# Routed stage: another order for the first layer's activations, the router's exponentials and the gated sums

## The chip, the core and the metric

One NeuronCore of a Trainium2 chip runs the whole program. The metric is the device time of one execution in microseconds (us), as the median of several executions.

## The reference

Two transformer layers run one after the other on 2 x 1024 rows of 256 numbers. Everything up to the last part (two attentions, a sparse feed-forward part) is untouched here. The last part, which the kernel calls the routed stage, is this:

```python
xr = layernorm(x).reshape(-1, D)
route_probs = softmax(xr @ wr.T)              # 8 experts
routes_k, indices_k = top_k(route_probs, 2)
gates = routes_k / sum(routes_k)
h = silu(xr @ w1.T)
h = silu(h @ w3.T)
h = h @ w2.T
out = zeros_like(xr)
for k in range(2):
    out = out.at[indices_k[:, k]].add(gates[:, k:k + 1] * h)
x = x + out
```

The indices name experts 0 to 7 and are used as row numbers of `out`, so that only its first 8 rows get anything: each is a sum over all rows, weighted by the gates.

## The kernel before

Rows are handled in 16 tiles of 128, four tiles to a chunk of 512, so there are four chunks (`d.NC`, the last one is `LAST`). Each stage is written by hand as one instruction list per engine; the lists meet only through semaphores, and each engine takes its own list strictly in order. So what sets the order of the work is the order of the calls in each engine's function. A wait holds up everything behind it on that engine.

Products in reduced-precision fp32 are made from a high part and a low part of each operand: three matmuls (high by high, high by low, low by high) stand for one. ScalarE (ACT) makes a high part by copying, VectorE (DVE) makes the low part by subtracting.

The stage before (`stage_queries`) has already normed, turned and split chunks 0 to 2 and prepared the weights. `stage_routed` (line 2116) has these pieces:

- `last_rows` (DVE) norms the last chunk; `turn_last` (TensorE, PE) transposes it into `ps_2` with 8 transposes; ACT copies the two halves to the high part (line 2263), `last_low` (DVE, line 2189) makes the low part.
- `route(c)` (PE) makes the router's 8 columns for four tiles: 6 matmuls of 8 columns for each tile. For chunks 0 to 2 it takes two matmuls of layer 1 (`layer1_terms`, line 2329, 512 columns) ahead of each tile, which makes the 24 of chunks 0 and 1. `route(LAST)` has no such matmuls between, and waits for the last chunk's low part (`lo_ok`).
- The router's softmax: DVE takes the maximum and subtracts it (lines 2241 and 2242, after all four `route` calls, `l_ps`), ACT makes the exponentials (line 2266, waits `lmax_ok`), and DVE goes on with `shares` (sums, quotients, the 8 largest), `places` (their positions) and `gates`, which releases `g_ok`.
- Layer 1 of a chunk: 12 matmuls on PE, then ACT applies Silu to each half (line 2274) and copies the high part (line 2276), then `low_h(c)` on DVE (line 2198). The buffers are double, by `c % 2`.
- Layer 2 of a chunk: 24 matmuls of 256 columns on PE, which wait for the low halves (`hl_ok`); ACT applies Silu from `ps_2` (line 2282), which releases `h2_ok`.
- `add_up(c)` (PE): four products of the gates with layer 2's rows (line 2359), all chunks summed into one bank `ps_a`. Then comes a short tail: a copy, two transposes, the product with w2, the addition to the first 8 rows and their way out.

ACT needs a table for each kind of function; changing it is an instruction of its own (`ACT_TABLE_LOAD`), which the compiler puts ahead of the first function that needs it. `warm` is an exponential of one column, whose result nobody uses, placed so that the exponentials' table is there early.

Of the kernel before, what the change touches and what calls it, by code (L numbers as in the profile page):

```python
# [23 lines left out]
P = 128  # L24
# [2091 lines left out]
def stage_routed(nc, d, io, keep, out):  # L2116


    with ExitStack() as ctx:
# [19 lines left out]
        acc = st.sb("acc", [NE, d.E])  # L2139
        acc_t = st.sb("acc_t", [P, d.KT, NE])  # L2140
        w = NormWork(st, TPC)
        warm = st.sb("warm", [P, 1])
        ps_th = [st.ps(f"ps_th{i}", [P, d.KT, d.CH]) for i in range(2)]
        ps_2 = st.ps("ps_2", [P, 2, d.CH])
        ps_l = st.ps("ps_l", [P, d.NT, NE])
# [4 lines left out]
            st.sem(n) for n in ("h_ps", "h1_ok", "hh_ok", "hl_ok", "l_ps", "lmax_ok", "ex_ok"))  # L2150
        h2_ps, h2_ok, g_ok, a_ps = st.sem("h2_ps"), st.sem("h2_ok"), st.sem("g_ok"), st.sem("a_ps")

        acc_ok, fin_ok, warm_ok = st.sem("acc_ok"), st.sem("fin_ok"), st.sem("warm_ok")
        out_tiles = out.rearrange("b (t p) e -> p (b t) e", p=P)
        HALVES = TPC // 2

        with nc.Block() as block:
# [12 lines left out]
            def _(dve):  # L2170
# [15 lines left out]
                def last_low():  # L2186
                    for k in range(d.KT):
                        dve.wait_ge(hi_ok, k + 1)
                        nc.vector.tensor_tensor(turned_rows(d, keep, 1, k, LAST * d.CH, d.CH), ps_2[:, k, :],  # L2189
                                                as_f32(turned_rows(d, keep, 0, k, LAST * d.CH, d.CH)),  # L2190
                                                ALU.subtract).then_inc(lo_ok, 1)

                def low_h(c):
                    if c >= 2:
                        dve.wait_ge(h2_ps, HALVES * (c - 1))
                    for m in range(d.KT):
                        dve.wait_ge(hh_ok, d.KT * c + m + 1)
                        nc.vector.tensor_tensor(h_lo[:, c % 2, m, :], h1[:, c % 2, m, :],  # L2198
                                                as_f32(h_hi[:, c % 2, m, :]), ALU.subtract).then_inc(hl_ok, 1)

                def spread(ap, n):
                    return ap.unsqueeze(2).to_broadcast([P, d.NT, n])
# [33 lines left out]
                last_rows()  # L2236
                dve.wait_ge(iota_ok, 1)
                nc.vector.tensor_copy(iota_f[:], iota_i[:])
                last_low()
                dve.wait_ge(l_ps, d.NC)  # L2240
                link(nc.vector.tensor_reduce(lmax[:], ps_l[:], AX.X, ALU.max))
                nc.vector.tensor_tensor(lg[:], ps_l[:], spread(lmax[:], NE), ALU.subtract).then_inc(lmax_ok, 1)
                shares()
                low_h(0)
                places()
                low_h(1)
                gates()
                for c in range(2, d.NC):
                    low_h(c)
                dve.wait_ge(a_ps, 1)  # L2250
                nc.vector.tensor_copy(acc[:], ps_a[0:NE, 0:d.E]).then_inc(acc_ok, 1)  # L2251
                dve.wait_ge(a_ps, 2)
# [4 lines left out]

            @block.scalar
            def _(act):
                norm_root(nc, act, w, 1)  # L2260
                for k in range(d.KT):
                    act.wait_ge(t_ps, k + 1)
                    nc.scalar.activation(turned_rows(d, keep, 0, k, LAST * d.CH, d.CH), ps_2[:, k, :], ACT.Copy).then_inc(hi_ok, 1)  # L2263
                nc.scalar.activation(warm[:], w.sd[:, 0:1], ACT.Exp, scale=0.0).then_inc(warm_ok, 1)
                act.wait_ge(lmax_ok, 1)
                nc.scalar.activation(ex[:], lg[:], ACT.Exp).then_inc(ex_ok, 1)  # L2266

                def layer1(c):
                    for m in range(d.KT):
                        act.wait_ge(h_ps, d.KT * c + m + 1)  # L2270
                        if c >= 2:
                            act.wait_ge(hl_ok, d.KT * (c - 1))
                            act.wait_ge(h2_ps, HALVES * (c - 1))
                        nc.scalar.activation(h1[:, c % 2, m, :], ps_th[c % 2][:, m, :], ACT.Silu).then_inc(h1_ok, 1)  # L2274
                        act.wait_ge(h1_ok, d.KT * c + m + 1)
                        nc.scalar.activation(h_hi[:, c % 2, m, :], h1[:, c % 2, m, :], ACT.Copy).then_inc(hh_ok, 1)  # L2276

                def layer2(c):
                    for j in range(HALVES):
                        act.wait_ge(h2_ps, HALVES * c + j + 1)  # L2280
                        t = TPC * c + 2 * j
                        nc.scalar.activation(h2[:, t:t + 2, :].rearrange("p t e -> p (t e)"), ps_2[:, j, :], ACT.Silu)\
                            .then_inc(h2_ok, 1)

                layer1(0)
                for c in range(d.NC):
                    if c + 1 < d.NC:
                        layer1(c + 1)
                    layer2(c)

            @block.tensor
            def _(pe):
# [69 lines left out]
                        ins.then_inc(a_ps, 1)  # L2362

                wide = itertools.chain(layer1_terms(0), layer1_terms(1))
                for c in range(LAST):
                    route(c)
                turn_last()
                route(LAST)
                for c in range(d.NC):
                    if 2 <= c + 1 < d.NC:  # L2370
                        layer1(c + 1)
                    layer2(c)
                    if c:
                        add_up(c - 1)
                add_up(d.NC - 1)
                pe.wait_ge(acc_ok, 1)
                for k in range(d.KT):
                    ins = nc.tensor.transpose(flat_l[:, k * NE:(k + 1) * NE], acc[:, k * P:(k + 1) * P],
# [77 lines left out]
```

## Time and profile before

| what | value |
|---|---|
| median of 3 runs | 1232.25 us (1230.89 to 1232.38) |
| the profiled execution's own time | 1228.95 us |
| its span | 1227.1 us |
| mean granted TensorE clock over the span | 0.958 |
| PE busy | 1083.5 us (88%) |
| DVE busy | 911.0 us (74%) |
| ACT busy | 628.5 us (51%) |
| routed stage, from its first matmul at 1171.08 us to the end of the span | 56 us |

All durations below are of the profiled execution. The time ahead of and behind the span is 1228.95 - 1227.1 = 1.85 us. Times of an instruction are counted from the start of the span. PE is the matrix engine's multiplication, which is pipelined: the record of a matmul is longer than its distance to the next one, so that distances from start to start are used. The granted clock is the share of the full TensorE clock (2.4 GHz) that the chip granted in a stretch: 1.00 is 2.4 GHz and 0.50 is 1.2 GHz.

### The profile page before, as it was taken

The page shows a single profiled execution, that of the slowest core. Times are in us where ns is not written, and L with a number is a line of the kernel's source. Part 1 is how long each engine was busy: PE and PEld are TensorE (multiplying, and loading weights), DVE is VectorE, ACT ScalarE, POOL GpSimd, SP SyncE. Part 2 cuts the span into 40 slices and gives each one's busy share as a digit, 9 for nine tenths or more (in the row PEclk, how much of TensorE's full clock was granted, in tenths as well). Part 3 has the DMA queues.
Part 4 walks back from the last instruction along what each step waited for, and adds up shares of the span by engine and source line. Part 5 has one row for each costly group of instructions (what it writes and reads, how often), then busy time and mean ns, then how long its engine had stood idle before and what let it go on. Part 6 is the DMA issues. An engine that isn't in the chain of part 4 may idle for free. (4 is left out here: it accounts for less than half of the span.)

```text
span 1227.1 us, 18400 instructions
## 1 busy us (share of the span) xinstructions
PE 1083.5 (88%) x7034; PEld 749.2 (61%) x7034; DVE 911.0 (74%) x1698; ACT 628.5 (51%) x1098; POOL 218.8 (18%) x173
## 2 busy tenths in 40 slices
PE   2979999999999987777867889999997899999978
PEld 2823333333333346666756768888886689888966
DVE  7778999999999604689898886565553878897833
ACT  2526878788787863775651223333333433433323
POOL 6004500000000001000033303000000744644400
PEclk9969999999999998998988999999997999999989
DMA  2771133033030010000000020110101000000010
GB/s 94 228 219 28 27 54 50 5 53 53 8 48 2 2 40 1 1 0 1 1 18 1 1 83 25 35 36 18 35 1 61 1 1 1 1 1 1 1 65 5
DMA packets 24850, 40.02 MB, mean 33 GB/s; under 512 B 3116, under 2 KB 12344, under 8 KB 24760
## 3 DMA queue, kind: packets, MB, share of 16 engines
q1 hardware_dynamic: 24760, 38.82, 13.2%
q8 instruction: 56, 0.92, 0.3%
q14 instruction: 34, 0.28, 0.1%
HBM read 28.06 MB, written 10.49 MB: 31 GB/s over the span
## 5 line engine op out<-in xcount | busy, mean ns | idle before, releaser
L668 DVE TENSOR_REDUCE att_mx<-att_ps_m 128x2 f32<-128x1024 f32 x256 | 310.9, 1225 | 23.3 <-PE att_ps_m L562 19.8
L651 ACT ACTIVATE att_prob<-att_ps_s 128x512 f32<-128x512 f32 x512 | 278.3, 596 | 80.3 <-PE att_ps_s L590 67.7
L606 PE MATMUL att_ps_o<-att_prob,v_rows 128*32 128x256 f32 (+1 forms) x1920 | 159.4, 405 | 0.0
L1885 POOL TENSOR_TENSOR qry_prod<-qry_qr,lin_ksum 128x512 f32<-128x512 f32 x64 | 93.1, 1457 | 302.7 <-ACT qry_qr L2006 291.5
L590 PE MATMUL att_ps_s<-qst,kst 50*128 50x512 f32 x512 | 127.9, 495 | 13.6 <-ACT att_prob L651 12.6
L590 PEld LDWEIGHTS att_ps_s<-qst,kst 50*128 50x128 f32 x512 | 48.1, 183 | 127.1 <-ACT att_prob L651 117.4
L562 PE MATMUL att_ps_m<-kst,qst 48*128 48x512 f32 x512 | 110.0, 424 | 8.7 <-DVE att_mx L668 7.0
L2006 ACT ACTIVATE qry_qr<-qry_ps_q 128x512 f32<-128x512 f32 x64 | 38.3, 599 | 132.4 <-PE qry_ps_q L153 118.9
L153 PE MATMUL qry_ps_o<-qry_m,qry_n_hi 128*128 128x256 f32 x512 | 98.6, 291 | 0.9 <-DVE qry_n_lo L1915 0.8
L1596 DVE SCALAR_TENSOR_TENSOR key_k_lo<-kf_ps,key_k_hi 128x512 fp32r<-128x512 f32 x64 | 44.2, 690 | 61.6 <-ACT key_k_hi L1674 61.0
L606 PEld LDWEIGHTS att_ps_o<-att_prob,v_rows 128*32 128x32 f32 x1920 | 38.1, 108 | 84.3 <-ACT att_prob L651 71.2
L153 PEld LDWEIGHTS qry_ps_o<-qry_m,qry_n_hi 128*128 128x128 f32 x512 | 77.7, 188 | 2.3 <-issue 1.8
L153 PE MATMUL qry_ps_o<-qry_m,qry_n_lo 128*128 128x256 f32 x256 | 71.3, 279 | 0.0
L1674 ACT ACTIVATE key_k_hi<-kf_ps 128x512 fp32r<-128x512 f32 x64 | 38.1, 597 | 62.6 <-PE kf_ps L153 55.4
L562 PEld LDWEIGHTS att_ps_m<-kst,qst 48*128 48x128 f32 x512 | 50.6, 193 | 22.4 <-DVE att_mx L668 18.4
L1915 DVE TENSOR_TENSOR qry_n_lo<-qry_ps_t,qry_n_hi 128x512 fp32r<-128x512 f32 x64 | 44.3, 691 | 24.3 <-ACT qry_n_hi L1995 22.5
L1905 DVE SCALAR_TENSOR_TENSOR qry_qn<-qry_rec,qry_qr 128x512 f32<-128x512 f32 x64 | 55.1, 861 | 2.2
L850 POOL MEMSET mlp_ones<- 128x128 f32 x1 | 0.2, 210 | 313.0 <-POOLq L502 313.0
L153 PE MATMUL kf_ps<-key_k_hi,kf_xk 128*128 128x512 f32 x128 | 45.9, 399 | 5.5 <-DVE key_k_lo L1596 5.5
L1900 DVE TENSOR_REDUCE qry_nrm<-qry_prod 128x8 f32<-128x512 f32 x64 | 43.7, 683 | 9.2 <-POOL qry_prod L1885 7.1
L153 PE MATMUL qry_ps_q<-qry_w_hi,kf_xt 128*128 128x512 f32 x128 | 47.2, 413 | 3.3 <-DVE qry_w_lo L1964 3.3
L1350 PE MATMUL kf_ps<-mlp_wp,ident 128*128 128x256 f32 x152 | 44.5, 456 | 5.4 <-ACT mlp_ws_t L1184 5.4
(409 smaller groups left out, 2330.2 us busy)
## 6 DMA issues: line engine op xcount, KB each, us to landing
qst<-qk_parts SPq DMA_DIRECT2D x48, 128.0 KB, 4.3
kst<-qk_parts SPq DMA_DIRECT2D x48, 128.0 KB, 6.5
qk_parts<-att_out SPq DMA_DIRECT2D x16, 256.0 KB, 4.5
qk_parts<-qk_lo SPq DMA_DIRECT2D x16, 256.0 KB, 4.6
residual<-L_attn_x SPq DMA_DIRECT2D x4, 512.0 KB, 5.9
lin_wq_raw<-L_attn_Wv SPq DMA_DIRECT2D x4, 512.0 KB, 3.6
lin_wq_raw<-L_attn_Wq SPq DMA_DIRECT2D x4, 512.0 KB, 5.5
lin_wq_raw<-L_attn_Wo SPq DMA_DIRECT2D x4, 512.0 KB, 3.9
```

What stands on the lines that cost most here:

```text
L153: ins = nc.tensor.matmul(out, a, b, start=first and n == 0, stop=last and n == len(terms) - 1)
L562: ins = nc.tensor.matmul(ps_m[:, n % 2, r, :], qst[g % RING][rows, v % NB, j, t * P:(t + 1) * P], kst[g % RING][rows, j, half * d.CH:(half ...
L590: ins = nc.tensor.matmul(ps_s[:, (n + r) % BANKS, :], kst[g % RING][rows, j, s * P:(s + 1) * P], qst[g % RING][rows, t, j, :], start=True, ...
L606: ins = nc.tensor.matmul(ps_o[32 * h:32 * h + 32, cols], vall[:, NS * b + s, h0 + h, :], prob[:, u % PR, h, cols], start=s == 0, stop=s == ...
L651: nc.scalar.activation(prob[:, u % PR, 2 * j + r, :], ps_s[:, (n + r) % BANKS, :], ACT.Exp).then_inc(exp_ok, 1)
L668: nc.vector.reduce_max(mx[:, v % 2, :, m], ps_m[:, n % 2], AX.X).then_inc(m_rd, 1)
L1350: nc.tensor.matmul(dst[:, 0:d.E], ident[:], wp[:, 1, :], start=True, stop=True)
L1596: nc.vector.scalar_tensor_tensor(out=k_lo[:, i % 2, :], in0=ps_k[:, i % 2, :], scalar=0.0, in1=as_f32(k_hi[:, i % 2, :]), op0=ALU.max, op1 ...
L1885: nc.gpsimd.tensor_tensor(prod[:, u % 2, :], qr[:, u % 2, :], ksum[:, b, cols(n)], ALU.mult).then_inc(pr_ok, 1)
L1900: link(nc.vector.tensor_reduce(nrm[:], prod[:, u % 2, :].rearrange("p (h e) -> p h e", e=HW), AX.X, ALU.add))
L1905: nc.vector.scalar_tensor_tensor(out=qn[:, u % 2, :].rearrange("p (h e) -> p h e", e=HW), in0=rec[:].unsqueeze(2).to_broadcast([P, HPB, HW ...
L1915: nc.vector.tensor_tensor(n_lo[:, u % 2, :], ps_t[:, u % 2, :], as_f32(n_hi[:, u % 2, :]), ALU.subtract).then_inc(n_ok, 1)
```

## The change

Only `stage_routed` is changed, and no arithmetic in it. On PE, `turn_last` comes after `route(1)` instead of after `route(2)`; layer 2 of a chunk comes ahead of layer 1 of the chunk two further on, not behind that of the next one; and the four `add_up` calls stand in two pairs, the first behind layer 2's third chunk, the second at the end. On ACT, layer 1 of chunk 0 comes ahead of the last chunk's high part, that of chunk 1 ahead of the exponentials, and later chunks of layer 1 follow layer 2 of the chunk two before; `warm` and its semaphore are gone. On DVE, the low halves of chunk 0 come ahead of `last_low`, those of chunk 1 ahead of `shares`, those of chunk 2 ahead of `places` and those of chunk 3 behind `gates`.

```diff
--- before.py
+++ after.py
@@ -2139,7 +2139,6 @@
         acc = st.sb("acc", [NE, d.E])
         acc_t = st.sb("acc_t", [P, d.KT, NE])
         w = NormWork(st, TPC)
-        warm = st.sb("warm", [P, 1])
         ps_th = [st.ps(f"ps_th{i}", [P, d.KT, d.CH]) for i in range(2)]
         ps_2 = st.ps("ps_2", [P, 2, d.CH])
         ps_l = st.ps("ps_l", [P, d.NT, NE])
@@ -2150,7 +2149,7 @@
             st.sem(n) for n in ("h_ps", "h1_ok", "hh_ok", "hl_ok", "l_ps", "lmax_ok", "ex_ok"))
         h2_ps, h2_ok, g_ok, a_ps = st.sem("h2_ps"), st.sem("h2_ok"), st.sem("g_ok"), st.sem("a_ps")
 
-        acc_ok, fin_ok, warm_ok = st.sem("acc_ok"), st.sem("fin_ok"), st.sem("warm_ok")
+        acc_ok, fin_ok = st.sem("acc_ok"), st.sem("fin_ok")
         out_tiles = out.rearrange("b (t p) e -> p (b t) e", p=P)
         HALVES = TPC // 2
 
@@ -2236,17 +2235,17 @@
                 last_rows()
                 dve.wait_ge(iota_ok, 1)
                 nc.vector.tensor_copy(iota_f[:], iota_i[:])
+                low_h(0)
                 last_low()
                 dve.wait_ge(l_ps, d.NC)
                 link(nc.vector.tensor_reduce(lmax[:], ps_l[:], AX.X, ALU.max))
                 nc.vector.tensor_tensor(lg[:], ps_l[:], spread(lmax[:], NE), ALU.subtract).then_inc(lmax_ok, 1)
+                low_h(1)
                 shares()
-                low_h(0)
+                low_h(2)
                 places()
-                low_h(1)
                 gates()
-                for c in range(2, d.NC):
-                    low_h(c)
+                low_h(3)
                 dve.wait_ge(a_ps, 1)
                 nc.vector.tensor_copy(acc[:], ps_a[0:NE, 0:d.E]).then_inc(acc_ok, 1)
                 dve.wait_ge(a_ps, 2)
@@ -2257,14 +2256,6 @@
 
             @block.scalar
             def _(act):
-                norm_root(nc, act, w, 1)
-                for k in range(d.KT):
-                    act.wait_ge(t_ps, k + 1)
-                    nc.scalar.activation(turned_rows(d, keep, 0, k, LAST * d.CH, d.CH), ps_2[:, k, :], ACT.Copy).then_inc(hi_ok, 1)
-                nc.scalar.activation(warm[:], w.sd[:, 0:1], ACT.Exp, scale=0.0).then_inc(warm_ok, 1)
-                act.wait_ge(lmax_ok, 1)
-                nc.scalar.activation(ex[:], lg[:], ACT.Exp).then_inc(ex_ok, 1)
-
                 def layer1(c):
                     for m in range(d.KT):
                         act.wait_ge(h_ps, d.KT * c + m + 1)
@@ -2282,11 +2273,22 @@
                         nc.scalar.activation(h2[:, t:t + 2, :].rearrange("p t e -> p (t e)"), ps_2[:, j, :], ACT.Silu)\
                             .then_inc(h2_ok, 1)
 
+                def last_high():
+                    for k in range(d.KT):
+                        act.wait_ge(t_ps, k + 1)
+                        nc.scalar.activation(turned_rows(d, keep, 0, k, LAST * d.CH, d.CH), ps_2[:, k, :], ACT.Copy)\
+                            .then_inc(hi_ok, 1)
+
+                norm_root(nc, act, w, 1)
                 layer1(0)
+                last_high()
+                layer1(1)
+                act.wait_ge(lmax_ok, 1)
+                nc.scalar.activation(ex[:], lg[:], ACT.Exp).then_inc(ex_ok, 1)
                 for c in range(d.NC):
-                    if c + 1 < d.NC:
-                        layer1(c + 1)
                     layer2(c)
+                    if c + 2 < d.NC:
+                        layer1(c + 2)
 
             @block.tensor
             def _(pe):
@@ -2362,17 +2364,20 @@
                         ins.then_inc(a_ps, 1)
 
                 wide = itertools.chain(layer1_terms(0), layer1_terms(1))
-                for c in range(LAST):
-                    route(c)
+                route(0)
+                route(1)
                 turn_last()
+                route(2)
                 route(LAST)
                 for c in range(d.NC):
-                    if 2 <= c + 1 < d.NC:
-                        layer1(c + 1)
+                    if c == LAST:
+                        add_up(0)
+                        add_up(1)
                     layer2(c)
-                    if c:
-                        add_up(c - 1)
-                add_up(d.NC - 1)
+                    if c + 2 < d.NC:
+                        layer1(c + 2)
+                add_up(2)
+                add_up(3)
                 pe.wait_ge(acc_ok, 1)
                 for k in range(d.KT):
                     ins = nc.tensor.transpose(flat_l[:, k * NE:(k + 1) * NE], acc[:, k * P:(k + 1) * P],
```

The order of the instructions moves as follows. The first place is ACT's list from the start of the stage on: `rt_sd` is the norm's root, `lin_xt0` the last chunk's high part, `rt_ps_th0` and `rt_ps_th1` the sums of layer 1's chunks 0 and 1, `rt_h_hi` their high part, `rt_ex` the exponentials, `rt_h2` layer 2's result. Before:

```order
L137 ACTIVATE rt_sd<-rt_ve 128x4
L2263 ACTIVATE lin_xt0<-rt_ps_2 128x512 x2
L2264 ACT_TABLE_LOAD
L2264 ACTIVATE rt_warm<-rt_sd 128x1
L2266 ACTIVATE rt_ex<-rt_lg 128x128
L2274 ACT_TABLE_LOAD
L2274 ACTIVATE rt_h1<-rt_ps_th0 128x512
L2276 ACTIVATE rt_h_hi<-rt_h1 128x512
```

There the exponentials stand ahead of all of layer 1, with two table loads. Now:

```order
L137 ACTIVATE rt_sd<-rt_ve 128x4
L2265 ACT_TABLE_LOAD
L2265 ACTIVATE rt_h1<-rt_ps_th0 128x512
L2267 ACTIVATE rt_h_hi<-rt_h1 128x512
...
L2279 ACTIVATE lin_xt0<-rt_ps_2 128x512 x2
L2265 ACTIVATE rt_h1<-rt_ps_th1 128x512
L2267 ACTIVATE rt_h_hi<-rt_h1 128x512
...
L2287 ACT_TABLE_LOAD
L2287 ACTIVATE rt_ex<-rt_lg 128x128
L2273 ACT_TABLE_LOAD
L2273 ACTIVATE rt_h2<-rt_ps_2 128x512 x2
```

Chunks 0 and 1 of layer 1 stand ahead of the exponentials, and there are three table loads: Silu's, the exponentials', Silu's again.

The second place is PE's list around the last chunk's transposes (`rt_xn` is its normed rows, `rt_ps_l` the router's columns, `rt_ps_th` layer 1's sums):

```order
-L2329 MATMUL rt_ps_th<-kf_xt_5561,rtw_wt_hi 128x512
-L2329 MATMUL rt_ps_th<-kf_xt_5560,rtw_wt_lo 128x512
+L2302 MATMUL rt_ps<-ident,rt_xn 128x128 x8
+L2331 MATMUL rt_ps_th<-kf_xt_5561,rtw_wt_hi 128x512
+L2331 MATMUL rt_ps_th<-kf_xt_5560,rtw_wt_lo 128x512
...
-L153 MATMUL rt_ps_l<-rtw_wr_hi,lin_xt 128x8
-L2300 MATMUL rt_ps<-ident,rt_xn 128x128 x8
-L153 MATMUL rt_ps_l<-rtw_wr_hi,lin_xt 128x8
+L153 MATMUL rt_ps_l<-rtw_wr_hi,lin_xt 128x8 x2
```

The transposes move four tiles earlier, so that four tiles of routing with their eight 512-column matmuls lie between them and the last chunk's routing. The last chunk's 24 matmuls of 8 columns now follow those of chunk 2 directly.

The third place is DVE's list (`rt_h_lo` is a chunk's low halves, `lin_xt` the last chunk's low part, `rt_lg` the logits less their maximum, `rt_esum` to `rt_best` the shares, `rt_idx` the places, `rt_gs` to `rt_gate` the gates). Now:

```order
L2237 CAST rt_iota_f<-rt_iota_i 128x8
L2197 TENSOR_TENSOR rt_h_lo<-rt_h,rt_h_hi 128x512 x2
L2188 TENSOR_TENSOR lin_xt<-rt_ps,lin_xt 128x512 x2
L2241 TENSOR_REDUCE rt_lmax<-rt_ps_l 128x16
L2242 TENSOR_TENSOR rt_lg<-rt_ps_l,rt_lmax 128x128
L2197 TENSOR_TENSOR rt_h_lo<-rt_h,rt_h_hi 128x512 x2
L2206 TENSOR_REDUCE rt_esum<-rt_ex 128x16
...
L2210 MAX rt_best<-rt_pr 128x8 x16
L2197 TENSOR_TENSOR rt_h_lo<-rt_h,rt_h_hi 128x512 x2
L2216 MAX_INDEX rt_idx<-rt_best,rt_pr 128x8 x16
L2221 TENSOR_TENSOR rt_gs<-rt_best 128x16
```

Before, the pairs of low halves stood behind `rt_best`, behind `rt_idx` and (four in a row) behind `rt_gate`; now one pair stands ahead of `lin_xt`, one behind `rt_lg`, one behind `rt_best`, and the last behind `rt_gate`.

## Rows read from the trace of the kernel before

**Rows 1.** Stretches: us, busy (x) of PE, PEld, DVE, ACT, POOL; granted clock; DMA share, GB/s

```profile
1182.00:1184.00 2.00, 2.00 (x17) 1.87 (x16) 0.00 (x0) 0.00 (x0) 0.00 (x0) 1.00 0.00 0
1189.00:1190.00 1.00, 1.00 (x7) 1.00 (x8) 0.00 (x0) 0.00 (x0) 0.00 (x0) 0.60 0.00 0
...
1199.00:1200.00 1.00, 1.00 (x9) 1.00 (x8) 1.00 (x3) 0.52 (x1) 0.00 (x0) 0.78 0.03 8
```

**Rows 2.** Chain that ended last, in order of time: start us, us, what

```profile
1184.85 0.53 PE rt_ps L2300 x4
...
1187.37 3.67 PE rt_ps_l L153 x24
...
1196.52 4.38 PE rt_ps L153 x24
1200.90 2.77 PE rt_ps_th L2329 x12
1203.67 2.80 PE rt_ps L153 x24
...
1215.86 3.00 PE rt_ps L153 x24
1218.86 3.56 PE rt_ps_a L2359 x16
```

**Rows 3.** Timeline of PE: start us, us, instruction, idle before and releaser

```profile
1177.07 0.40 PE L2329 MATMUL rt_ps_th<-kf_xt,rtw_wt_lo 128*128 128x512 f32 x1
...
1187.37 0.27 PE L153 MATMUL rt_ps_l<-rtw_wr_hi,lin_xt 128*128 128x8 f32 x1 [1.57 <-DVE lin_xt L2189]
1187.50 0.25 PE L153 MATMUL rt_ps_l<-rtw_wr_lo,lin_xt 128*128 128x8 f32 x1
...
1189.18 0.36 PE L153 MATMUL rt_ps_l<-rtw_wr_lo,lin_xt 128*128 128x8 f32 x1
...
1196.52 0.58 PE L153 MATMUL rt_ps<-rtw_wt_hi,rt_h_hi 128*128 128x256 f32 x1 [5.49 <-DVE rt_h_lo L2198]
```

**Rows 4.** Timeline of PE in the queries stage, around eight transposes

```profile
1146.59 1.04 PE L2062 MATMUL qry_ps_f<-ident,lin_wq_raw 128*128 128x128 f32 x8
1147.38 0.48 PE L153 MATMUL qry_ps_q<-qry_w_hi,lin_xt 128*128 128x512 f32 x1
```

**Rows 5.** Timeline of ACT: MLP stage, then routed stage

```profile
454.20 1.28 ACT L137 ACT_TABLE_LOAD   x1
462.21 0.21 ACT L137 ACTIVATE mlp_sd<-mlp_ve 128x4 f32<-128x4 f32 x1 [6.73 <-DVE mlp_ve L115]
...
1191.72 0.31 ACT L2266 ACTIVATE rt_ex<-rt_lg 128x128 f32<-128x128 f32 x1 [3.72 <-DVE rt_lg L2242]
1192.04 1.28 ACT L2274 ACT_TABLE_LOAD   x1
1193.34 0.60 ACT L2274 ACTIVATE rt_h<-rt_ps_th 128x512 f32<-128x512 f32 x1
1193.97 0.63 ACT L2276 ACTIVATE rt_h_hi<-rt_h 128x512 fp32r<-128x512 f32 x1
```

**Rows 6.** Timeline of DVE in the routed stage

```profile
1191.07 0.29 DVE L2241 TENSOR_REDUCE rt_lmax<-rt_ps_l 128x16 f32<-128x128 f32 x1 [3.75 <-PE rt_ps_l L153]
...
1192.06 0.29 DVE L2207 TENSOR_REDUCE rt_esum<-rt_ex 128x16 f32<-128x128 f32 x1 [0.37 <-ACT rt_ex L2266]
...
1194.70 0.69 DVE L2198 TENSOR_TENSOR rt_h_lo<-rt_h,rt_h_hi 128x512 fp32r<-128x512 f32 x1 [0.52 <-ACT rt_h_hi L2276]
...
1196.38 0.08 DVE L2217 MATCH_VALUE_LOAD rt_idx<-rt_best,rt_pr 128x8 f32 x1
...
1198.68 1.30 DVE L2198 TENSOR_TENSOR rt_h_lo<-rt_h,rt_h_hi 128x512 fp32r<-128x512 f32 x2
1199.90 0.19 DVE L2222 TENSOR_TENSOR rt_gs<-rt_best 128x16 f32<-128x16 f32 x1
...
1201.83 0.29 DVE L2234 TENSOR_TENSOR rt_gate<-rt_oh,rt_rgs 128x128 f32<-128x128 f32 x1
```
## The prediction

> **What bounds the kernel now.** I read the busy time by stretch first, then the chain that ended last, then PE's own timeline, and ACT's and DVE's for the prices. The change touches only the end of the program, so only what lies behind 1171 us matters. In the stretches [rows 1] the reader is to see that PE is busy without a break at full clock (1.00) while the router's columns are mixed with 512-column matmuls (1182 to 1184), that the granted clock falls to half in the microsecond from 1189 (mean 0.60), and that it is back to full only in the one from 1199 (mean 0.78). The chain [rows 2] runs on PE but for two breaks. PE's timeline [rows 3] gives both: 1.57 us at 1187.37, where PE waits for DVE's low part of the last chunk, and 5.49 us at 1196.52, where it waits for DVE's low halves of layer 2's first chunk. So two waits (7.06 us) and some 10 us at half clock bound this stretch; behind 1200.90 PE runs solidly to 1222.42 (1218.86 + 3.56). DVE and ACT matter only where they end those waits.
>
> **Part 1: the transposes move four tiles earlier, the exponentials behind layer 1's first two chunks.** If neither wait comes back, PE's work can simply be laid end to end. All of routing but the last chunk ends where the transposes begin, at 1184.85 [rows 2]. The prices:
>
> - eight transposes, 0.79 us: from their first start to the next matmul's in the queries stage [rows 4]; in the routed stage they are followed by a wait, so that their distance isn't seen there;
> - 24 matmuls of 8 columns at full clock: fifteen start distances from 1187.50 to 1189.18 [rows 3], 0.112 each, so 2.69 us;
> - a chunk of layer 2: 2.80 us, 3.00 behind `add_up`; of layer 1: 2.77 us; two `add_up` together: 3.56 us [rows 2].
>
> Laid out: transposes and routing to 1185.64, `route(LAST)` to 1188.33, layer 2 of chunk 0 to 1191.13, layer 1 of chunk 2 to 1193.90, layer 2 of chunk 1 to 1196.70, layer 1 of chunk 3 to 1199.47, layer 2 of chunk 2 to 1202.27, two `add_up` to 1205.83, layer 2 of chunk 3 to 1208.83, two `add_up` to 1212.39. Before, the same point was 1222.42. The tail behind it is not touched, so the term is **-10.03 us**.
>
> **Does every wait hold?** The margins, by the other engines' rows [rows 5, 6]:
>
> - `lo_ok` at 1185.64. Four tiles of routing (eight wide matmuls at 2.77/12 = 0.231, 24 narrow ones at 0.112) take 4.5 us, so the transposes end at about 1181.1; a copy (0.63) and two subtractions (0.69 each) later, at 1183.1, the low part is there. Margin 2.5 us. What is queued behind this wait is all of PE; it no longer waits there.
> - Low halves of chunk 0 at 1188.33. Its last sums end at 1177.47 [rows 3]; Silu (0.60), copy (0.63) and DVE (0.69) give 1179.4. Margin 9 us: this was the 5.49.
> - DVE now stands at `l_ps` with chunk 1's low halves behind it. From 1188.33 the maximum and the subtraction take 0.65 (1191.07 to 1191.72, where ACT begins), so the exponentials start at 1189.0; the two low halves take 1.30, to 1190.3. PE asks for them at 1193.90. Margin 3.6 us.
> - ACT: exponentials to 1189.35, Silu's table (1.28) to 1190.65, two Silus of layer 2 (0.60 each) to 1191.85; PE wants the first half of `ps_2` again at 1193.90. Margin 2.6 us. The load for the exponentials is free: a load ahead of a waiting function runs at once, as at 454.20, where its function began at 462.21 after 6.73 us of waiting [rows 5]; here that is from about 1186.2, under `route(LAST)`. So the third table load, which the change adds, costs nothing, and would cost 1.28 us without layer 2's chunk 0 beside it.
> - `gates`: shares 2.1 us (1192.06 to 1194.18) to 1192.4; chunk 2's low halves, whose sums end at 1193.90, to 1195.9; places 2.3 (1196.38 to 1198.68) to 1198.2; gates 2.2 (1199.90 to 1202.12) to 1200.4 [rows 6]. PE asks at 1202.27. Margin 1.8 us, the narrowest. Chunk 3's low halves follow at 1201.7, wanted at 1205.83.
>
> Dropping `warm` saves ACT one small function that lay beside routing: nothing. No DMA moves and neither SP's nor POOL's list changes: nothing. Moving `add_up` costs PE no work, and saves one change between the two kinds of products, which is in the layout (one 3.00 rather than two such slower steps).
>
> **Part 2: the clock.** The waits go, but not the matmuls of 8 columns. The rows show [rows 1, 3] that the clock fell after 1.57 us of idling and 1.8 us of these matmuls alone, while the same kind mixed with wide ones kept full clock. Now they run alone for 2.69 us plus the last mixed tile's six (0.67), 3.36 us with no wide matmul between. No row shows just this without an idle stretch, so it is bounded. Below: the clock stays, 0. Above: all 24 narrow ones at half clock (twice 2.69, so 2.69 more) and layer 2's chunk 0 slowed as before, by 4.38 - 2.80 = 1.58 [rows 2]: 4.27 us. I take **+1.58**: it is nearest to the row of the same chunk, which stood behind the same 24 matmuls, and the clock returned 2.9 us after it resumed (1196.52, back within the microsecond from 1199). I leave the narrow ones at full clock, since before they had most of theirs.
>
> **Sum.** -10.03 + 1.58 = -8.45 us. Against the profiled execution's own 1228.95 that is 1220.5. The median of the runs is 1232.25, 3.3 us above the profiled one; the same difference gives **1223.8 us**.
>
> **Rivals.**
>
> 1. *The clock stays up.* PE never idles, and the narrow matmuls alone don't lower it. For: half of what preceded the fall, the idling, is gone. Against: the 1.8 us just ahead of it were narrow matmuls at an unbroken pace. 1232.25 - 10.03 = 1222.2 us.
> 2. *The clock falls early*, at the start of the narrow matmuls, and layer 2 starts cold: the upper bound, 1232.25 - 10.03 + 4.27 = 1226.5 us. For: the narrow stretch is now longer than the one before the fall. Against: nothing idle lies in front.
> 3. *ACT's tables lie on the path.* There are three loads now, not two. If both later loads wait behind `lmax_ok` and each holds ACT for twice its 1.28 us, the first Silu of layer 2 ends at 1189.0 + 2.56 + 0.31 + 2.56 + 0.60 = 1195.0, 1.1 us after PE asks: 1224.9 us. Against: the function behind the load of 1192.04 began at 1193.34, 0.02 us after its end, and the load at 454.20 did not wait [rows 5]. The Trainium skill, "ScalarE: Activation LUTs", section "What ACT_TABLE_LOAD costs", speaks for this rival: it gives a switch 1283 ns of load and about 1380 ns of drain, 2.66 us together, and would have functions of one set done together. By that rule, with both loads behind the wait, an estimate is 1.3 us late and 1225.1 us; the trace agrees with the load's duration and shows no drain.
> 4. *The waits only move*, and the change doesn't do what its order says: a new wait as long as the gain. The gates at `add_up` are the place with the least room (1.8 us), and PE's layer 2 of chunk 3 stands behind them. They would have to come 10 us late to bring no change, where the whole chain from the exponentials is 11.4 us long (1189.0 to 1200.4). 1232 us, within 0.2%.
> 5. *Slower*: the clock, once down, stays down to the end. Behind 1188.33 lie 24.06 us of PE work at full clock; twice that is 24 us more: 1246 us. It decides from 20 us at half clock on, which eat the 10.03. For: the clock did stay low for 10 us here. Against: 5.49 us of those were idle, and layer 2 brought it back in 2.9 us without a pause of its own; behind 1188.33 PE has none.
>
> **Chances.** Forecast 0.55, clock stays up 0.15, clock falls early 0.15, tables 0.07, waits only move 0.05, slower 0.03. What can be told from no change here is 0.2%, 2.5 us. The forecast and rivals 1 to 3 are all faster by more: 0.92; within 0.2%: 0.05; slower: 0.03. The range reaches from rival 1 to rival 2, and on both sides by the distance of the three runs shown (1232.38 - 1230.89 = 1.5 us): 1220.7 to 1228.0. It leaves out rivals 4 and 5.
>
> **What would show it.** Right: PE has no idle stretch over 0.3 us between the stage's first matmul and the copy of `ps_a`; `route(LAST)` follows chunk 2's routing directly; layer 2's chunk 0 starts near 1188.3; ACT shows the exponentials' table load well ahead of them and Silu's beside layer 2's chunk 0; the granted clock falls once, near 1188 to 1190, and is back before 1194. The first `add_up` record comes at about 1202.3. Wrong: idle time of PE released by `h2_ok` (rival 3) or by DVE's gates (rival 4), no fall of the clock (rival 1), or chunk 0 of layer 2 and more at 0.50 (rivals 2 and 5).

## The result and the profile after

The changed kernel takes 1222.51 us (median of 7 runs, 1220.79 to 1226.06), the one before 1232.25 us (median of 7 runs beside them, 1228.57 to 1237.46). The ratio is 0.9929, with a 95% interval of 0.9914 to 0.9945: 8.7 us less by the ratio, between 6.8 and 10.6 (the medians themselves differ by 9.7). Forecast were 8.45 us less and 1223.8 us. The profiled execution of the changed kernel took 1222.51 us, with a span of 1220.7; that of before took 1228.95 us. One execution of the version "exponentials first" below (2060.94 us) and one of the kernel before beside it (5639.81 us) were slow and stay out of the ratios.

Below, "the stage" is the stretch from the first matmul of routing to the end of the last gated sums. Before it went from 1171.08 to 1222.42, 51.34 us; now it goes from 1171.41 to 1216.04 (1212.49 + 3.56), **44.63 us**. What lies behind it takes 4.7 us in both. First the chain that ended last, of the changed kernel, from the transposes on (start us, us, what):

```profile
1180.63 0.95 PE rt_ps L2302 x8
...
1185.45 5.04 PE rt_ps_l L153 x30
1190.49 4.31 PE rt_ps L153 x24
1194.80 2.79 PE rt_ps_th L2331 x12
1197.59 2.80 PE rt_ps L153 x24
1200.39 2.75 PE rt_ps_th L2331 x12
1203.14 2.80 PE rt_ps L153 x24
1205.94 3.55 PE rt_ps_a L2361 x16
1209.49 3.00 PE rt_ps L153 x24
1212.49 3.56 PE rt_ps_a L2361 x16
```

Every piece is PE's and each begins where the last one ends: the two breaks of [rows 2, 3] are gone. The 30 narrow matmuls (24 of the last chunk and the last mixed tile's six) take 5.04 us, and layer 2's first chunk 4.31, nearly the 4.38 of [rows 2]; from there on every price is that of [rows 2]. Then the stretches of the changed kernel (stretch; us; busy us of PE, PEld, DVE, ACT, POOL; granted clock; DMA share; GB/s):

```profile
1171.41:1216.04 44.63, 44.63 (x280) 37.80 (x280) 16.57 (x89) 19.96 (x31) 0.11 (x1) 0.92 0.13 45
1185.00:1186.00 1.00, 1.00 (x10) 0.92 (x9) 0.00 (x0) 0.51 (x1) 0.00 (x0) 1.00 0.00 0
1186.00:1187.00 1.00, 1.00 (x10) 1.00 (x9) 0.00 (x0) 0.95 (x3) 0.00 (x0) 0.80 0.00 0
1187.00:1190.00 3.00, 3.00 (x16) 3.00 (x15) 0.00 (x0) 1.05 (x1) 0.00 (x0) 0.50 0.00 0
1190.00:1193.00 3.00, 3.00 (x15) 3.00 (x15) 2.37 (x7) 1.59 (x2) 0.00 (x0) 0.50 0.00 0
1193.00:1194.00 1.00, 1.00 (x9) 1.00 (x8) 0.97 (x13) 0.60 (x1) 0.00 (x0) 0.79 0.00 0
```

PE is busy for all 44.63 us. Yet the clock falls to half at about 1186.6 and is back at about 1193.4. The mean of 0.80 means 0.4 us at half, 0.79 the same; with the six between, 6.8 us at half clock. In the kernel before it was 10.2 us by the same reckoning: 0.8 and 0.4 us in the first and the last microsecond by [rows 1], and nine at 0.50 between them, 5.49 us of it spent idle. Its whole stage, columns as above, has a mean clock of 0.90:

```profile
1171.08:1222.42 51.34, 44.27 (x280) 36.82 (x280) 16.83 (x89) 18.66 (x31) 0.10 (x1) 0.90 0.12 39
```

The fall now comes in the middle of the narrow matmuls, and PE's timeline shows their pace change (start us, us, instruction):

```profile
1186.43 0.43 PE L153 MATMUL rt_ps_l<-rtw_wr_hi,lin_xt 128*128 128x8 f32 x2
...
1186.93 0.57 PE L153 MATMUL rt_ps_l<-rtw_wr_hi,lin_xt 128*128 128x8 f32 x2
1187.36 0.35 PE L153 MATMUL rt_ps_l<-rtw_wr_lo,lin_xt 128*128 128x8 f32 x1
```

The two that begin from 1186.93 on take 0.43 us to the next row's start, 1187.36, where two took 0.22 at full clock (0.112 each, by [rows 3]). ACT's timeline, the exponentials and the first Silu of layer 2:

```profile
1186.76 1.28 ACT L2287 ACT_TABLE_LOAD   x1
1191.18 0.31 ACT L2287 ACTIVATE rt_ex<-rt_lg 128x128 f32<-128x128 f32 x1 [3.13 <-DVE rt_lg L2242]
1191.51 1.28 ACT L2273 ACT_TABLE_LOAD   x1
1193.29 0.60 ACT L2273 ACTIVATE rt_h<-rt_ps 128x512 f32<-128x512 f32 x1 [0.51 <-PE rt_ps L153]
```

The exponentials' table is loaded 4.4 us ahead of its function. Silu's load ends at 1192.79, and then ACT still waits 0.51 us for PE: the third load is hidden. DVE's last row of the gates:

```profile
1203.77 0.29 DVE L2233 TENSOR_TENSOR rt_gate<-rt_oh,rt_rgs 128x128 f32<-128x128 f32 x1
```

The gates are there at 1204.06, and the chain has PE ask for them at 1205.94.

### The profile page after: what moved, and what is told of

It is laid out like the page before. It is cut to its first block and busy times, and to the rows that moved or that the text cites. A ratio compares the mean times of both kernels' runs of the same rounds, so it can differ in the third digit from the quotient of the medians.

```text
span 1220.7 us, 18398 instructions
## 1 busy us (share of the span) xinstructions
PE 1085.2 (89%) x7034; PEld 751.1 (62%) x7034; DVE 910.9 (75%) x1698; ACT 629.6 (52%) x1098; POOL 218.8 (18%) x173
## 3 DMA queue, kind: packets, MB, share of 16 engines
q1 hardware_dynamic: 24760, 38.82, 13.5%
```

## The experiments

The theory: the two waits were all that the order cost, each moved part removes one of them, and what is left over PE's bare work is the clock, which the narrow matmuls lower by running alone. The rivals: an ACT or DVE chain takes part of the gain (tables, gates); or the clock fell for another reason than the narrow matmuls. For each run the table gives the stage in its profile, PE's waits within it, the time at half clock by the means of its stretches, and the runs; the bare work is 41.46 us, as measured below in the kernel that never leaves full clock, and "clock" is what is left of the stage over it and the waits. That kernel has another order, so "clock" is good to a few tenths of a microsecond: in the kernel before and in "gated sums each" it holds some 0.3 us of PE's order there (from the end of layer 2's first chunk on, the kernel before takes 21.5 us, the changed one 21.25), and the 0.15 us in the last row has no half clock in it. Each ratio is to runs of the kernel before made beside it; their medians are 1231.16 to 1231.31 us, but for the row "changed" (1232.25).

| kernel | stage us | waits | clock | at half | median us | ratio (95%) |
|---|---|---|---|---|---|---|
| before | 51.34 | 7.06 | 2.8 | 10.2 | 1232.25 | 1 |
| before, once more | 51.29 | 7.07 | 2.8 | 10.2 | 1231.65 | 1.0007 (0.9992 to 1.0021) |
| changed | 44.63 | 0 | 3.2 | 6.8 | 1222.51 | 0.9929 (0.9914 to 0.9945) |
| changed, once more | 44.56 | 0 | 3.1 | 6.8 | 1221.53 | 0.9924 (0.9911 to 0.9937) |
| changed, third time | 42.96 | 0 | 1.5 | 3.4 | 1222.28 | 0.9923 (0.9906 to 0.9940) |
| transposes late | 47.97 | 1.57 | 4.9 | 10.2 | 1225.89 | 0.9962 (0.9942 to 0.9982) |
| exponentials first | 50.80 | 5.50 | 3.8 | 13.7 | 1232.36 | 0.9999 (0.9985 to 1.0013) |
| both of these | 51.01 | 7.06 | 2.5 | 10.2 | 1231.37 | 1.0003 (0.9993 to 1.0012) |
| gated sums each | 48.59 | 3.71 | 3.4 | 6.8 | 1229.44 | 0.9989 (0.9973 to 1.0005) |
| wide in the last chunk | 41.46 | 0 | 0 | 0 | 1221.55 | 0.9927 (0.9908 to 0.9947) |
| the same, once more | 41.46 | 0 | 0 | 0 | 1221.05 | 0.9921 (0.9909 to 0.9933) |
| the same, third time | 41.44 | 0 | 0 | 0 | 1221.64 | 0.9921 (0.9905 to 0.9938) |
| layer 2 in the last chunk | 41.81 | 0.20 | 0.15 | 0 | 1221.33 | 0.9911 (0.9893 to 0.9929) |

### The transposes late

PE turns the last chunk behind `route(2)` again; all else stays as changed.

```diff
                 route(1)
-                turn_last()
                 route(2)
+                turn_last()
                 route(LAST)
```

> The changed kernel with one part undone: the eight transposes of the last chunk come behind chunk 2's routing again. My theory (the first wait is worth its own length): PE waits again for the last chunk's low part, about 1.6 us in front of the last chunk's routing, and the clock falls all the same; 1.6 to 2.5 us slower than the changed kernel, some 7 us faster than the one before. Rival (the wait lay beside the clock's loss and costs nothing by itself): within 0.5 us of the changed kernel.

From the chain, the narrow matmuls and what follows; then PE's timeline at the wait:

```profile
1189.01 4.81 PE rt_ps_l L153 x24
1193.81 5.33 PE rt_ps L153 x24
1199.14 3.13 PE rt_ps_th L2331 x12
```

```profile
1189.01 0.27 PE L153 MATMUL rt_ps_l<-rtw_wr_hi,lin_xt 128*128 128x8 f32 x1 [1.57 <-DVE lin_xt L2188]
```

The wait is back at the very length of [rows 3], 1.57 us. The stage is 3.3 us longer than the changed one, though: the clock, down for 10.2 us instead of 6.8, slows the narrow matmuls (4.81 for 24), layer 2's first chunk (5.33) and part of layer 1's next (3.13). So the early transposes are worth 1.57 us of waiting and, in this pair of profiles, 1.8 us of clock. That is more than the 1.6 to 2.5 us expected, and the runs agree: by the ratios they lose 4 to 5 us against the changed kernel, and gain 4.7 rather than 7 on the one before. How much of the clock's part belongs to the wait isn't shown by one profile, since those of the changed kernel itself differ by 1.6 us.

### The exponentials first

ACT's and DVE's lists have layer 1's activations and the low halves behind the exponentials again. PE's order stays as changed.

```diff
-                low_h(0)
                 last_low()
...
-                low_h(1)
                 shares()
-                low_h(2)
+                low_h(0)
                 places()
+                low_h(1)
                 gates()
+                low_h(2)
                 low_h(3)
...
                 norm_root(nc, act, w, 1)
-                layer1(0)
                 last_high()
-                layer1(1)
                 act.wait_ge(lmax_ok, 1)
                 nc.scalar.activation(ex[:], lg[:], ACT.Exp).then_inc(ex_ok, 1)
+                layer1(0)
+                layer1(1)
```

> The changed kernel with ACT's and DVE's order undone (exponentials, shares, places and gates ahead as before), PE's new order kept. My theory: PE waits again 5 to 5.5 us in front of layer 2's first chunk (maximum, exponentials, a table load, four activations and a subtraction in a row), so it is 5 to 6 us slower than the changed kernel and only 2 to 3.5 us faster than the one before. Rival (PE's order alone, above all the later gated sums, brings most of it): at most 2 us slower than the changed kernel.

PE's timeline at the wait, and from the chain the narrow matmuls and layer 2's first chunk:

```profile
1199.85 0.58 PE L153 MATMUL rt_ps<-rtw_wt_hi,rt_h_hi 128*128 128x256 f32 x1 [5.50 <-DVE rt_h_lo L2197]
```

```profile
1189.33 5.03 PE rt_ps_l L153 x30
...
1199.85 5.01 PE rt_ps L153 x24
```

The second wait is back, again at its old length (5.49 in [rows 3], 5.50 here). The time is that of before, 0.9999, where a kernel 2 to 3.5 us faster was expected. The next run, "both of these", differs from this one by the transposes alone. Against it the 1.57 us wait is gone, but the stage is only 0.2 us shorter (50.80 and 51.01): 1.3 us is given back to the clock (3.8 against 2.5 us), which is at half for 13.7 us instead of 10.2. In this pair of profiles, a wait saved ahead of a longer one was worth next to nothing; the runs (0.9999 and 1.0003) can't tell that from the full 1.57 us.

### Both of these

The two edits together leave only PE's order of the layers and the paired gated sums.

> The kernel before with only PE's new order behind the routing (layers two chunks apart, gated sums in pairs); transposes, ACT's and DVE's order as before. My theory: both waits (1.6 and 5.5 us) are there, and the pairing alone gives nothing but one slower step less; stage 51 to 51.4 us against 51.3, time within 0.1% of the kernel before. Rival (the later sums give PE work to do ahead of the gates and so gain by themselves): 1 us or more faster than the kernel before.

PE's timeline at its two waits:

```profile
1190.54 0.27 PE L153 MATMUL rt_ps_l<-rtw_wr_hi,lin_xt 128*128 128x8 f32 x1 [1.57 <-DVE lin_xt L2188]
...
1199.12 0.58 PE L153 MATMUL rt_ps<-rtw_wt_hi,rt_h_hi 128*128 128x256 f32 x1 [5.49 <-DVE rt_h_lo L2197]
```

Both waits are those of [rows 3], and the time is that of before (1.0003). PE's new order alone brings nothing; the stage is 0.3 us shorter than before, the part of PE's order named above, which the runs can't show.

### Gated sums behind each chunk

The four gated sums stand behind layer 2 of the next chunk, as before the change; the other parts stay.

```diff
                 for c in range(d.NC):
-                    if c == LAST:
-                        add_up(0)
-                        add_up(1)
                     layer2(c)
+                    if c:
+                        add_up(c - 1)
                     if c + 2 < d.NC:
                         layer1(c + 2)
-                add_up(2)
                 add_up(3)
```

> The changed kernel with the gated sums one chunk at a time again, each behind the next chunk of layer 2, as before the change; all else new. My theory: the gates are the narrowest place, PE reaches the first sum some 3.7 us before they are there and waits so long; 3 to 4 us slower than the changed kernel. Rival (the pairing is cosmetic, as PE's work is the same): within 0.4 us of the changed kernel.

PE's timeline at the first gated sum; then the stretches around it, with columns as above; then two pieces of the chain, and from that of the kernel before the chunk of layer 1 in the same place:

```profile
1207.72 3.08 PE L2361 MATMUL rt_ps_a<-rt_h,rt_gate 128*8 128x256 f32 x8 [3.71 <-DVE rt_gate L2233]
```

```profile
1207.00:1208.00 1.00, 0.28 (x2) 0.15 (x3) 0.60 (x3) 0.00 (x0) 0.00 (x0) 1.00 0.00 0
1208.00:1211.00 3.00, 3.00 (x9) 0.95 (x8) 0.00 (x0) 0.00 (x0) 0.00 (x0) 0.55 0.00 0
1211.00:1212.00 1.00, 1.00 (x4) 0.79 (x5) 0.00 (x0) 0.00 (x0) 0.00 (x0) 0.65 0.00 0
```

```profile
1210.80 3.37 PE rt_ps_th L2331 x12
...
1216.97 1.82 PE rt_ps_a L2361 x8
```

```profile
1208.29 2.95 PE rt_ps_th L2329 x12
```

PE comes to the first gated sum before DVE has the gates, and waits 3.71 us, just what was expected. What was not: the clock falls a second time right behind that wait (0.55 in the three microseconds from 1208), so that eight gated products take 3.08 us instead of the later 1.82, and a chunk of layer 1 3.37 instead of 2.95. So rival 4's place, the gates, is where the changed order is nearest to a wait, and the pairing of the sums is what keeps it away. The stage is 4.0 us longer than the changed one, as expected; the runs lose more than that, 6.9 us by the medians, and the rest is not in this profile's stage. The run's gain over before (0.11%) is too small to be told from none.

### Wide matmuls among the last chunk's narrow ones

Layer 1 of chunk 2, twelve matmuls of 512 columns, is not run behind layer 2's first chunk but spread over the last chunk's routing, three to a tile. Its waits and its amount of work are the same.

```diff
-                        for _ in range(2 if c < LAST else 0):
+                        for _ in range(2 if c < LAST else 3):
                             next(wide, None)
...
-                wide = itertools.chain(layer1_terms(0), layer1_terms(1))
+                wide = itertools.chain(layer1_terms(0), layer1_terms(1), layer1_terms(2))
...
                     layer2(c)
-                    if c + 2 < d.NC:
-                        layer1(c + 2)
+                    if c == 0:
+                        layer1(LAST)
```

> The changed kernel, with the 12 wide matmuls of layer 1's chunk 2 put between the last chunk's narrow ones, three ahead of each tile, and layer 1's chunk 3 behind layer 2's chunk 0; same instructions, other order. My theory (narrow matmuls alone lower the clock, with no idling needed): the granted clock stays at 1.00 from 1172 us to the end, layer 2's chunk 0 takes 2.80 us and not 4.31, and the time is 1.5 to 3.3 us below the changed kernel's. Rival (something else lowers it: the transposes, or what PE did before): the clock falls near the same place and the time is within 0.5 us of the changed kernel's. A second rival: the gates come later than the first gated sum and PE waits there, which eats up to 1 us.

> The version with layer 1's chunk 2 between the last chunk's narrow matmuls, on the same chip as the changed kernel. My theory: the stage stays at full clock and takes 41.4 to 41.6 us, as laid end to end; the median is 1.5 to 3.3 us below that of the changed kernel. Rival: the clock that is saved here is lost elsewhere, or the stage's time was no more than luck; medians within 0.7 us.

> The version with layer 1's chunk 2 between the last chunk's narrow matmuls once more. My theory: stage 41.4 to 41.6 us at full clock; the median over all runs of the three calls 1 to 3 us below the changed kernel's. Rival: the medians stay within 0.7 us, so that something ahead of the stage goes against it.

The stretches of the third of these runs, columns as above, and its chain:

```profile
1174.00:1190.00 16.00, 16.00 (x116) 14.77 (x115) 3.59 (x8) 7.18 (x11) 0.00 (x0) 1.00 0.24 80
1190.00:1212.00 22.00, 22.00 (x148) 17.16 (x147) 10.54 (x68) 10.64 (x18) 0.00 (x0) 1.00 0.00 1
```

```profile
1189.74 0.81 PE rt_ps_th L2331 x3
1191.11 2.91 PE rt_ps L153 x24
1194.02 2.77 PE rt_ps_th L2331 x12
...
1208.94 3.56 PE rt_ps_a L2361 x16
```

All three profiles show the clock at 1.00 throughout and the stage at 41.44 to 41.46 us. The narrow matmuls are the same 24; only the company differs. In all nine profiles in which they run alone, the clock falls within them or in layer 2's first chunk behind them; in these three, and in the fourth below, it doesn't. So they do lower the clock when they run alone, and that is what separates the changed kernel's 44.63 us from its bare work. This version also measures the forecast's layout of 41.31 us: right to 0.15, which is what the transposes took above their price (0.95 us here, 0.79 taken from [rows 4]).

The runs gain less than the stage does, and less than the 1 to 3.3 us expected. The medians of the three sets of runs are 1221.05 to 1221.64, those of the changed kernel 1221.53 to 1222.51; within each of the two sets that held both, the difference is 0.5 and 0.6 us, less than the runs of one kernel differ, as the rivals of the second and third expectation had it. Why stays open. It may lie in the executions without a profile, whose stages nobody knows: the changed kernel may lose less clock in them. Or it lies ahead of the stage, in code that no edit touches: over the 13 profiles the stage starts anywhere from 1171.05 to 1176.75 us, and the granted clock of the first 900 us is 0.96 in all those that start before 1172 and 0.95 in all that start after 1174. That the whole program gains by this version is not shown. One pair of profiles has nearly the same start: the changed kernel's third run (1173.08, span 1220.7) and the second of this version (1173.00, span 1219.1). There the spans differ by 1.6 us, and the stages by 1.5.

### The changed kernel and the one before, once more

Both unchanged, to see how much the stage itself varies.

> The changed kernel, unchanged, on one chip with the next one. What it asks: whether the stage (first matmul to the end of the gated sums, 44.6 us in the profile after, of which 6.8 us at half clock) always loses the clock. My theory: yes, as the 24 narrow matmuls are always there, for one or two spells of 3.4 us as all spells in these traces; stage 43.0 to 45.0 us. Rival (a matter of luck): a profile without half clock in the stage, 41.4 us.

> The changed kernel once more, beside the two versions with dense matmuls between the narrow ones and the kernel before, all on one chip. Open is why the stage of the wide version is 3.1 us shorter in two profiles each while the medians differ by 0.5 us. My theory: the start of the stage varies by several us from execution to execution (1171.1 to 1176.7 us in the profiles so far), by half-clock spells that lie ahead of it and that no change here touches, and medians of six runs carry that; stage 43.0 to 44.8 us here, half clock in it. Rival: without a half-clock spell in the stage in most executions (41.4 us), the profiles so far being unlucky.

> The kernel before, for a second profile of it. My theory: both waits at the same lengths (1.57 and 5.49 us), about 10 us at half clock, stage 51.0 to 51.8 us. Rival: the half-clock spell differs by one spell of 3.4 us between executions, so that the stage is some 1.5 us longer or shorter and the difference of one profile from another is no measure of the change.

The second profile of the changed kernel repeats the first, with the same mean clock of 0.92 over the stage (below) and 5.07 us for the 30 narrow matmuls, and that of before is the same to 0.05 us.

```profile
1174.77:1219.33 44.56, 44.56 (x280) 37.81 (x280) 16.57 (x89) 19.97 (x31) 0.10 (x1) 0.92 0.14 45
```

The changed kernel's third is 1.6 us shorter. Its stretches, then its chain:

```profile
1173.08:1216.04 42.96, 42.96 (x280) 36.17 (x280) 16.57 (x89) 19.98 (x31) 0.11 (x1) 0.96 0.14 47
1189.00:1190.00 1.00, 1.00 (x12) 1.00 (x11) 0.00 (x0) 0.70 (x1) 0.00 (x0) 1.00 0.00 0
1190.00:1191.00 1.00, 1.00 (x10) 1.00 (x10) 0.58 (x3) 0.00 (x0) 0.00 (x0) 0.99 0.00 0
1191.00:1194.00 3.00, 3.00 (x17) 3.00 (x16) 2.90 (x20) 2.19 (x3) 0.00 (x0) 0.50 0.00 0
1194.00:1195.00 1.00, 1.00 (x7) 0.95 (x7) 0.24 (x4) 0.15 (x1) 0.00 (x0) 0.81 0.00 0
```

```profile
1187.11 3.25 PE rt_ps_l L153 x30
1190.35 4.46 PE rt_ps L153 x24
```

Here the clock falls only when the narrow matmuls are over: they take 3.25 us, and layer 2's first chunk pays alone (4.46 instead of 2.80). This is nearly the forecast's clock term, 1.5 us, in one profile of three. The profile with the gated sums behind each chunk, whose PE list is the same up to there, has it so too (3.24 and 4.46). In the other two of the changed kernel the clock falls 15.2 us into the stage rather than 17.9, and the term is twice as large. What makes it fall early or late with the same instructions isn't settled by these runs.

### Layer 2 in the last chunk

Instead of layer 1's chunk 2, layer 2's chunk 0 is spread over the last chunk's routing, six matmuls of 256 columns to a tile.

```diff
-                        for _ in range(2 if c < LAST else 0):
-                            next(wide, None)
+                        for _ in range(2):
+                            next(wide if c < LAST else dense, None)
...
-                def layer2(c):
+                def layer2_terms(c):
...
+                                yield
...
+                dense = layer2_terms(0)
...
-                    layer2(c)
+                    if c:
+                        layer2(c)
```

> The changed kernel with layer 2's chunk 0 (24 matmuls of 256 columns, six ahead of each tile) between the last chunk's narrow ones; the rest in the changed kernel's order. My theory (any dense work between the narrow ones keeps the clock): no half clock in the stage, 41.4 to 41.8 us, at most 0.3 us of waiting at the gated sums, since the logits come 2.8 us later and the margin was 1.8 us by the rows of before. Rival (only 512-column matmuls keep it): half clock as in the changed kernel, 43 to 45 us. A second rival: PE waits 0.5 us or more for layer 2's first activation or for the gates.

The stretch behind 1190, then ACT's timeline, then PE's:

```profile
1190.00:1212.00 22.00, 21.80 (x145) 17.67 (x145) 10.55 (x68) 10.77 (x18) 0.00 (x0) 1.00 0.00 1
```

```profile
1194.24 1.28 ACT L2273 ACT_TABLE_LOAD   x1
1195.54 1.08 ACT L2273 ACTIVATE rt_h<-rt_ps 128x512 f32<-128x512 f32 x2
```

```profile
1196.28 0.35 PE L153 MATMUL rt_ps<-rtw_wt_hi,rt_h_hi 128*128 128x256 f32 x1 [0.20 <-ACT rt_h L2273]
```

Matmuls of 256 columns keep the clock up as well. But with layer 2's first chunk done before the exponentials, only layer 1's next chunk (2.8 us) stands between them and the chunk of layer 2 that wants `ps_2` free again. The exponentials, Silu's table load and the Silu behind it no longer fit beside that: PE waits 0.20 us for Silu. This is rival 3's place, reached once its cover is gone. The stage is 41.81 us, 0.35 more than with layer 1 there.

## Why the prediction was right, and which step was not

**The total.** Forecast 8.45 us less, measured 8.7 (6.8 to 10.6), and 9.4 and 9.5 us in the two repetitions (0.0076 and 0.0077 of some 1231). The stage itself gains 6.7 us in two profiles and 8.3 in the third. So the total came out as forecast while part of its working did not: a stage that gains 6.7 us would have given 1225.5 us, and that the median lies within 1.3 us of 1223.8 is in part luck. The 1 to 3 us between the stage's gain and the runs' stay open; the stage's start, which varies by 5.7 us, could hold them.

**The waits: -10.03 us.** Right. PE has no idle stretch in the stage, and where the clock is kept at full the laid-out work takes 41.46 us where 41.31 were worked out. Each wait comes back at its old length when its part is undone (1.57, 5.50). But the parts don't add: undoing the early transposes costs 3.3 us of stage, undoing the exponentials' place 6.2, undoing the pairs 4.0, 13.5 together where the change as a whole brings 6.7. Of the 6.8 us between, 3.7 is a wait that the kernel before does not have: the 3.71 us at the gates, which came in time before because PE stood 5.49 us ahead of layer 2 (1202.12 by [rows 6], wanted at 1206.47). The other 3 us are clock. The prediction treated a wait as a thing of its own length; in these profiles each also came with another time at half clock, though one profile of each can't say how much of that is the wait's.

**The margins.** Right: the gates have 1.88 us (1205.94 less 1204.06), where 1.8 were forecast, and neither rival 4 nor rival 5 came. What lies behind the narrow matmuls was late: layer 2's first chunk began at 1190.35 rather than 1188.3 (by its first record), the first gated sums at 1205.87 rather than 1202.3. The gates were late by as much as the gated sums (1204.06 for 1200.4), since DVE and ACT follow PE's slower matmuls, and so the margin held.

**The tables.** Right: the third load lies under layer 2's first chunk, and the exponentials' load ran 4.4 us ahead of its function. By the Trainium skill, "ScalarE: Activation LUTs", section "What ACT_TABLE_LOAD costs", a drain of about 1380 ns would go with each switch. No row shows one: in the changed kernel Silu began 0.50 us behind its load's end, and its row names PE as what it waited for; in the last experiment it began 0.02 us behind (1194.24 + 1.28, and 1195.54).

**The clock: +1.58 us.** This is the term that was mis-sized. The step that failed is "I leave the narrow ones at full clock, since before they had most of theirs". Two of three profiles have the fall within the narrow matmuls, at about 1186.6 in the first: the 30 take 5.04 us where 3.36 (30 of 0.112) were counted, 1.7 us more, and layer 2's first chunk 1.51 more, 3.2 us in all. The clock fell once, as forecast, and was back at 1193.4, before 1194; but it fell at 1186.6 rather than between 1188 and 1190. The size of layer 2's part was right. Part of the other stood in [rows 2]: before, the 24 narrow ones took 3.67 us where 2.69 were counted, and the prediction put that 1.0 us at nothing. The rest the rows of before could not give: there the clock fell 1.8 us into the narrow matmuls, here 1.15, and part of the time at half clock fell into the 5.49 us that PE waited anyway. That is why removing 7.06 us of waits took only 3.4 us off the time at half clock and nothing off its price: 2.8 us before (0.3 of it PE's order), 3.2 now. Between the forecast's 1.58 and rival 2's 4.27, the truth lay at 1.5 to 3.2: in two of three profiles it was rival 2, a clock that falls early, at three quarters of its price.

The idle stretch, which spoke for rival 1 by its absence, turned out not to be needed. The Trainium skill, "TensorE: Matmul & The Clock Gate", section "Why this matters for your kernels", names long idle gaps of PE between bursts of matmuls as what loses the clock. The wait of 3.71 us agrees with it (3.4 us at half clock follow), but here the clock also fell with PE never idle.

## What to carry to other kernels

An engine order in which a ready result waits behind an unrelated one (here the low halves behind the router's exponentials) is found from PE's releasers, and its gain is worked out by laying PE's work end to end, as long as every other engine's margin is checked. Price each wait together with what the clock does behind it: a repaired wait may be worth more than its length, and one ahead of another wait next to nothing (one profile of each here). Undoing parts one by one can bring up waits that the first kernel never had, so their costs need not add up to the whole. Where narrow matmuls must run, put dense ones between them: this took 1.5 to 3.2 us off the stage, at no cost in work; in the whole program's medians, 0.5 us, it could not be told from the spread.

## What the hardware showed that was not expected

- The clock fell to half in an unbroken run of 30 matmuls of 8 columns, with PE busy for 1.00 of every microsecond, in two of the changed kernel's three profiles, and just behind it in the third. With three matmuls of 512 columns, or six of 256, to each six narrow ones it stayed at 1.00 in four profiles of four.
- The same instructions in the same order had 3.4 us at half clock in one execution and 6.8 in two others.
- A wait of 3.71 us in the middle of dense work (the gated sums each) was followed by 3.4 us at half clock; the 0.20 us wait of the last experiment by none.
